# Two attention layers and a mixture of experts on one core: an order of steps computed anew, and three queue details

## The reference

```python
x = L0_attn_x                                    # (2, 1024, 128) float32
x = layernorm(x + attn(x))                       # 8 heads of 16, causal, plus head_scale * q_proj * k_proj
# ffn(x), inside the last line:
#   x = x + mla_attention(rmsnorm(x))            # 16 heads of 8, rotary, latent of 64, causal
#   x = x + moe(rmsnorm(x))                      # argmax over 4 experts, 128 -> 512 -> 128, relu
x = layernorm(x + ffn(x))
```

## Time and profile before

| | us |
|---|---|
| median of 3 runs | 563.38 (559.97 to 565.47) |
| profiled execution | 565.1 |
| its span | 563.4 |
| TensorE busy | 480.2 (85%) |
| VectorE busy | 371.9 (66%) |
| ScalarE busy | 323.6 (57%) |
| mean granted TensorE clock | 0.95 |

### The profile page before, as it was taken

The page is one execution under the profiler, slowest core; times in us unless marked ns, Lnnn a source line. Parts: engine busy times, 40 slices in busy tenths (PEclk is TensorE's granted clock), DMA queues, the critical chain, the costliest instruction groups (busy, mean ns, idle before and its releaser), DMA issues.

```text
span 563.4 us, 10237 instructions
## 1 busy us (share of the span) xinstructions
PE 480.2 (85%) x3749; PEld 223.4 (40%) x3764; DVE 371.9 (66%) x690; ACT 323.6 (57%) x488; POOL 179.8 (32%) x249
## 2 busy tenths in 40 slices
PE   5576799998899989888797998848888988999993
PEld 3242233444442333333232333312554443367762
DVE  4286977788877889688888788866356721233343
ACT  3422156576676668867685776715456677843331
POOL 9830131237554237634030222452202304601000
PEclk9977889999999999999999799976899999999998
DMA  3894030306112002012010102031000000100010
GB/s 96 214 210 132 2 96 23 94 1 243 45 56 65 25 5 83 28 52 65 17 43 9 52 3 58 6 98 45 6 12 15 8 12 20 30 1 0 20 38 20
DMA packets 31571, 28.83 MB, mean 51 GB/s; under 512 B 8017, under 2 KB 27857, under 8 KB 31250
## 3 DMA queue, kind: packets, MB, share of 16 engines
q1 hardware_dynamic: 30626, 26.34, 16.3%
q0 software_dynamic: 896, 1.84, 1.4%
HBM read 19.27 MB, written 9.31 MB: 51 GB/s over the span
## 4 chain that ended last, share of the span: by engine, by line
PE 58%; ACT 10%; DVE 10%; SPq 8%; issue 5%; DMA 4%; POOL 3%; ACTq 1%; another core or an unknown queue 0%; DVEq 0%; POOLq 0%
PE ps L1407 15%; PE ps L1390 10%; ACT pr L1607 7%; PE ps L1370 7%; DVE mparts L1887 6%; PE ps L1486 5%; PE ps L1542 5%; SPq L1018 4%; PE ps L1472 3%; SPq L1088 3%; DMA qs<-nparts 2%; PE ps L1466 2%; PE ps L1586 2%; PE ps L1574 2%; PE ps L1418 2%
## 5 line engine op out<-in xcount | busy, mean ns | idle before, releaser
L1887 DVE TENSOR_REDUCE mparts<-ps 128x2 f32<-128x1024 f32 (+3 forms) x240 | 260.4, 1114 | 83.0 <-PE ps L1370 78.5
L1607 ACT ACTIVATE pr<-ps 128x1024 f32<-128x1024 f32 (+1 forms) x240 | 221.2, 939 | 142.9 <-PE ps L1390 140.6
L1407 PE MATMUL ps<-pr,vs 128*32 128x512 f32 (+3 forms) x1152 | 124.4, 506 | 9.1 <-ACT pr L1607 5.7
L1390 PE MATMUL ps<-qs,ks 64*128 64x512 bf16 (+7 forms) x561 | 102.1, 339 | 21.1 <-DMA qs<-nparts 11.3
L1370 PE MATMUL ps<-ks,qs 61*128 61x512 bf16 (+7 forms) x576 | 108.7, 348 | 4.0 <-DVE mparts L1887 1.9
L1208 POOL TENSOR_SCALAR_AFFINE_SELECT pr<-pr 128x512 f32<-128x512 f32 x96 | 60.7, 635 | 156.5 <-ACT pr L1607 156.3
L1390 PEld LDWEIGHTS ps<-qs,ks 64*128 64x128 bf16 (+1 forms) x576 | 31.5, 96 | 106.7 <-issue 41.6
L1370 PEld LDWEIGHTS ps<-ks,qs 61*128 61x128 bf16 (+1 forms) x576 | 35.5, 101 | 33.3 <-ACT pr L1607 11.0
L1407 PEld LDWEIGHTS ps<-pr,vs 128*32 128x32 f32 x1152 | 23.6, 108 | 48.5 <-issue 30.1
L1711 ACT ACTIVATE work<-ps,b 128x512 f32<-128x512 f32 x32 | 21.8, 685 | 29.7 <-PE ps L1542 28.2
L1363 PE MATMUL ps<-cmask,identb 64*128 64x128 bf16 (+1 forms) x96 | 23.4, 244 | 11.8 <-DVE mparts L1887 4.8
(11 more groups left out here) (174 smaller groups left out, 563.5 us busy)
## 6 DMA issues: line engine op xcount, KB each, us to landing
qs<-scr0q SPq DMA_DIRECT2D x48, 64.0 KB, 2.4
qs<-scr1q SPq DMA_DIRECT2D x84, 32.0 KB
ks<-scr1k SPq DMA_DIRECT2D x84, 32.0 KB
ks<-scr0k SPq DMA_DIRECT2D x36, 64.0 KB, 2.3
scr0q<-parts SPq DMA_DIRECT2D x4, 384.0 KB, 3.1
scr0k<-parts SPq DMA_DIRECT2D x4, 384.0 KB, 3.6
scr1q<-parts SPq DMA_DIRECT2D x4, 384.0 KB, 2.5
scr1k<-parts SPq DMA_DIRECT2D x4, 384.0 KB, 2.7
```

The source lines that it names most:

```text
L1390: last = pe.matmul(to[:, k, h, :], keys(F, 3, 2 * k + h0 + h, j * P, P), queries(F, 3, 2 * k + h0 + h, qb * 512 + lo, n), start=True, stop ...
L1407: last = pe.matmul(ps[VW * h:VW * (h + 1), PVB, lo:lo + n], vs[:, F % VSLOTS, j, VW * h:VW * (h + 1)], pr[:, st % PSLOTS, h, 0:n], start=( ...
L1607: act.activation(heads, scores_at(F, v), ACT.Exp, scale=GROUPS[F][0].scale).then_inc(exped, 1)
L1887: dve.tensor_reduce(heads, maxes_at(F, u), AX_X, ALU.max).then_inc(taken, 1)
```

## The change

- `rows` of the second attention: one transfer writes both halves of the partitions, so 3 transfers in place of 6.
- A load of group F may be planned only behind `rows` of group F - 2.
- Of the first keys' two halves the second is on GpSimd's queue now, the first on SyncE's.
- At most two scatters are open: scatter t waits until scatter t - 2 has landed.
- `tile_out` and `tile_relu` read the tile's expert number into a register ahead of their wait for the step before them, no longer behind it.
- `hidden` c = 0 waits for its input explicitly (its own engine's earlier `gate` had waited for it before).
- Durations, places, weights of the planner and the limit of side banks (3 to 4) are other numbers, so nearly all of the 1401 steps stand elsewhere in the list.

```diff
-MOST = {"scores": 2, "row maxima": 2, "turns": 2, "side": 3}
+MOST = {"scores": 2, "row maxima": 2, "turns": 2, "side": 4}
...
-FIRST = [[(-2.0, -1.5), (-1.6, -1.1)], [(-0.5, 0.0), (-0.1, 0.4)]]
+FIRST = [[(-2.0, -1.5), (-1.6, -1.1)], [(-0.69, -0.19), (0.0, 0.5)]]
...
-URGENT = 0.6
-FEED, BACKLOG = 0.2, 2.0
-SP_IDLE = 5.0
+URGENT = 0.83
+FEED, BACKLOG = 0.36, 3.0
+SP_IDLE = 3.3
...
-         "combine": (DVE, 0.3), "rows": (SP, 1.0), "mask": (POOL, 0.64), "evac": (ACTE, 0.6), "y": (PE, 1.14),
+         "combine": (DVE, 0.3), "rows": (SP, 2.4), "mask": (POOL, 0.64), "evac": (ACTE, 0.59), "y": (PE, 1.14),
...
+def queue_of_load(F, k, half):
+
+    if F == 0 and k == 1:
+        return POOL if half == POOL_HALF else SP
+    return ACTE if F in ON_ACT else SP
...
+POOL_HALF = 1
+ON_ACT = ()
...
         if F >= SLOTS:
-            out.append(("scores", F - SLOTS, NU - 1))
+            out += [("scores", F - SLOTS, NU - 1), ("rows", F - SLOTS + 1, 2)]
...
-            return 48 * (F + 1) + 48 * max(0, F + 1 - ATT[0].groups)
+            return 48 * (F + 1)
...
                     if at.n == 1:
-                        for pair_of in range(2):
-                            row = HALF * (pair_of + 1) - MAXIMA + p
-                            sp.dma_start(qs[row:row + 1, F % SLOTS, 0:2 * T],
-                                         nparts[2 * TB * pair_of:2 * TB * (pair_of + 1), place, p, :]).then_inc(rows_in, 16)
+                        row = HALF - MAXIMA + p
+                        sp.dma_start(qs[row:row + HALF + 1:HALF, F % SLOTS, 0:2 * T], nparts[0:n, place, p, :]).then_inc(rows_in, 16)
...
+                if t >= 2:
+                    pool.wait_ge(scattered[t % 2], 16 * (t // 2))
...
                 elif kind == "hidden":
                     b, i, c = args
+                    if c == 0:
+                        pe.wait_ge(done["feat"], nth("feat", "hat1", b, i))
...
                 elif kind == "tile_out":
                     s, j = args
+                    e = pe.value_load(expert_of[0:1, j:j + 1], min_val=0, max_val=E - 1)
                     pe.wait_ge(done["tile_relu"], nth("tile_relu", s, j))
                     wait_bank(*step)
-                    e = pe.value_load(expert_of[0:1, j:j + 1], min_val=0, max_val=E - 1)
...
                 elif kind == "tile_relu":
                     s, j = args
+                    if j == 0:
+                        act.wait_ge(done["places"], nth("places", s))
+                    e = act.value_load(expert_of[0:1, j:j + 1], min_val=0, max_val=E - 1)
                     act.wait_ge(done["tile_hidden"], nth("tile_hidden", s, j))
                     if j >= 2:
                         act.wait_ge(done["tile_out"], nth("tile_out", s, j - 2))
-                    e = act.value_load(expert_of[0:1, j:j + 1], min_val=0, max_val=E - 1)
```

More of the change, by code:

```diff
@@ L276, in halves_of_load @@
     return (0, 1) if F in HALVED else (2,)
+LOADED_AHEAD = 1.9
 def wanted():
@@ L299, in wanted @@
         for half in halves_of_load(F):
-            add("loads", [(max(-1.05, F - 1.9) + 0.01 * half, ("load", F, k, half)) for k in range(2)])
+            add("loads", [(max(-1.05, F - LOADED_AHEAD) + 0.01 * half, ("load", F, k, half)) for k in range(2)])
     add("loads", [(F - 0.5, ("copy_v", F)) for F in range(NF)])
@@ L356 @@
+         "latent": (PE, 0.97), "lat_copy": (ACTE, 0.38), "lat_moments": (DVE, 1.55), "lat_norm": (ACTE, 1.75),
+         "lat_turn": (PE, 0.58), "lat_feat": (ACTE, 0.77), "square": (ACTE, 0.62), "square_sum": (DVE, 0.7),
+         "hat": (POOL, 1.1), "x12": (POOL, 1.3), "gate": (PE, 0.95), "pick": (DVE, 2.1), "hidden": (PE, 0.88),
+         "relu": (ACTE, 0.68), "expert": (PE, 0.92), "pick_up": (DVE, 1.4), "layer_norm": (DVE, 1.4), "out": (SP, 0.5),
          "copy_v": (POOL, 0.66), "pads": (POOL, 3.6), "ones": (POOL, 4.0), "halves": (POOL, 1.7), "weights": (SP, 5.2), "moe_weights": (SP, 1.1),
@@ L380, in costs @@
     if kind == "load":
-        queue = POOL if step[1:3] == (0, 1) else SP
-        return [(queue, 0.55 * len(PRODUCTS) if queue == POOL else 0.34 * len(PRODUCTS) * (1 + GROUPS[step[1]][0].n))]
+        queue = queue_of_load(*step[1:])
+        return [(queue, 0.55 * len(PRODUCTS) if queue == POOL else (0.47, 0.68)[GROUPS[step[1]][0].n] * len(PRODUCTS))]
     if kind == "b2_parts":
@@ L393, in costs @@
     if kind == "expert" and step[4] == 0:
-        return [(PE, 1.45)]
+        return [(PE, 1.23)]
     return [COSTS[kind]]
@@ L735, in order @@
             end[step] += LANDS_LATER[kind]
-        if step[:3] == ("load", 0, 1):
-            end[step] += POOL_LANDS
+        if kind == "load" and costs(step)[0][0] != SP:
+            end[step] += POOL_LANDS if costs(step)[0][0] == POOL else AFTER_ISSUE[SP]
         if kind == "max":
@@ L895, in build @@
         order_made, rows_set = sem("order_made"), sem("rows_set")
-        scattered, collected_in = sem("scattered"), [sem(f"collected_in{i}") for i in range(2)]
+        scattered, collected_in = [sem(f"scattered{i}") for i in range(2)], [sem(f"collected_in{i}") for i in range(2)]
         sorted_in = [sem(f"sorted_in{p}") for p in range(-(-(TB + E - 1) // PIECES))]
@@ L1054, in sorted_rows @@
                 j = slice(PIECES * p, min(PIECES * p + PIECES, rows_of_tiles(s)))
-                sp.wait_ge(scattered, 16 * len(tokens_of(s)))
+                for n in range(2):
+                    sp.wait_ge(scattered[n], 16 * len(tokens_of(s)) // 2)
                 if p == 0:
@@ L1099, in _ @@
                     store(*args)
-                elif kind == "load" and args[:2] != [0, 1]:
+                elif kind == "load" and queue_of_load(*args) == SP:
                     load(sp, *args)
@@ L1251, in _ @@
                 kind, *args = step
-                if kind == "load" and args[:2] == [0, 1]:
+                if kind == "load" and queue_of_load(*args) == POOL:
                     load(pool, *args)
@@ L1608, in _ @@
                                    scale=GROUPS[F][0].scale).then_inc(exped, 1)
+                elif kind == "load" and queue_of_load(*args) == ACTE:
+                    load(act, *args)
                 elif kind == "evac":
```

18 lines of the change are left out of this document (7 added, 11 removed).

## The result

| | before | after |
|---|---|---|
| median of 4 runs, us | 563.05 (559.97 to 565.47) | 526.76 (524.31 to 528.18) |
| span of the profiled execution | 563.4 | 525.4 |
| TensorE busy | 480.2 | 470.2 |
| TensorE standing still | 83.2 | 55.2 |

The changed kernel takes 0.935 of the time, with an interval of 0.930 to 0.941. I had said 546 us and 535 to 562. Of the 38 us between the two spans 28 are standstill and 10 are busy time. The work is the same (3764 weight loads in both), so I put these 10 down to the clock, whose mean was 0.950 before and 0.971 after.

A forecast was written before the change was run, and what follows sets the result against it. TensorE, busy 85% of the span, was taken as the bound, so order costs time only where it waits or its clock is down. Terms of -4, -4, -6, -1.5, -4 and 0 took 565.1 us to 545.6, said as 546; range 535 to 562.

The forecast's parts named there:

- 1, start: Start: fewer bytes ahead of the first keys and earlier maxima rows, first scores near 43 us; -4 us (0 to -8).
- no-change rival: Whole kernel: what is gained at these places is waited for elsewhere, group 1's maxima come later; about 563 us, 13%.
- 2, three transfers: Maxima rows of eight groups: three transfers instead of six shorten TensorE's waits for them; -4 us (+3 to -5.6).
- term 4: Clock at group 7: the dip follows a wait for maxima that gets 1.6 us shorter; -1.5 us (0 to -3).
- 3, group 9: Group 9, from `places` to its scores: maxima rows issued ahead of a load, shorter hole; -6 us (-1 to -12).
- 5, tiles: Tiles: expert number read ahead of the wait, so 0.78 us before `tile_out` lie beside it; -4 us (0 to -6.8).
- 6, the rest of the order: All other moved steps: same work, TensorE's time filled in the middle, so no gain; 0 us (-6 to +8).
- Slower: Maxima rows of eight groups: each narrow transfer lands late and the clock falls at other groups; 575 us, 5%.
- half-of-it rival: Start stays DMA-bound and VectorE's standstills return at group 9, other gains hold; -10.5 us, 554.6 us, 13%.

The follow-up runs named there:

- order alone: Changed kernel with its three code edits (three transfers, two open scatters, early reads) undone, new planner numbers and rules kept: 538.26 us, ratio 0.955.
- code alone: Kernel before, with its old planner numbers and order, plus the three code edits (three transfers, two open scatters, early reads): 545.82 us, ratio 0.970.

## Why the prediction was wrong, point by point

- **1, start (-4): too small, and by another path.** The first maximum came at 25.94 (I said 26), the issue of the first rows at 39.58 (I said 37.7), the first scores at 46.62 (I said near 43). That is -2.1 at the place I watched. The lead at group 0's cut was 9.3 us, half of it standstill (25.4 to 20.8) and half busy time (70.1 to 65.5 with 428 and 422 weight loads, the clock 0.87 to 0.92). It goes with the second rows, issued 8.1 us sooner. My sum followed the first rows only. The no-change rival had even named the shift that helped, four instead of seven maxima of group 1 ahead of group 0's second ones, and counted it as a loss.
- **2, three transfers (-4): -9.5 in the old order, -7 in the new.** The issue got as short as said (from 3.67 us for six, in the runs above, to 1.59 for three). The landing did not get longer. I priced only TensorE's five waits for the rows; the clock dip of group 7 went with them (term 4, -1.5), and group 9 gained some 3 us more. The sum of 2 and 4 was -5.5. A reading was off too: the 1.76 us of landing in the earlier trace rows begin with the start of the last issue, not behind it.
- **3, group 9 (-6): the place was right.** From `places` to the scores 10.6 us for 17.8, where I built up 12.6 (with 2.1 us of landing, which the earlier trace rows do not have: they give 1.76, the last issue included). VectorE's standstills did not return; the load or the scatters each would have sufficed. The two open scatters, at 0 by me, brought 3.9 us in the old order, where they took the standstill away. In the new order they were not tried alone; of the 11.5 us between order alone and the changed kernel about 2 are left after the other two edits.
- **5, tiles (-4): 6.5 in the old order, 2.6 in the new.** In the old one 5.9 of the 6.8 us of waits at `tile_out` went; in the new one 3.9 of 5.9 went and 1.8 us of "issue" are left. The Trainium skill gives TensorE a queue of 64 instructions ("TensorE: Matmul & The Clock Gate", table of specifications), and from it I had taken that the read would cost nothing, 6.8 us in the sum. The old order comes near that, the new one does not.
- **6, the rest of the order (0): this is the step that failed.** I put it at nothing because the work is the same and TensorE "has 93% of its time filled in the middle". The first is no reason: the same work waited less. The second was misread: between the cuts of groups 0 and 8 TensorE was busy 243.6 of 273.1 us, 89%, and stood still for 29.5. With the order alone it stands still for 17.2 there, with the code alone for 24.2. In time the order alone brought 8.8 us outside the start and group 9, 6.0 of them in groups 1 to 3, where I had no term at all. With the 5.2 us that term 1 was short at the start and the 2.1 us by which the order alone passed term 3 at group 9, that is 16 of the 18.5 us that the sum lacked. What went were many short waits, of which I had summed none but those for the rows.
- **Clock.** TensorE's busy time fell by 10 us. I had 1.5 for group 7 and a bound at group 9. With the missing records counted, the order alone took 5.4 of it (482.0 to 476.6), the code edits on top 4.2 (to 472.4). The order alone still has mean clocks of 0.89 and 0.94 at groups 6 and 7, which are 0.94 and 1.00 after.
- **Slower (5%).** Between 192.5 and 196.6 us the trace after counts 102 packets under 512 bytes for three transfers, 34 each, against 32 each before (192 in six). 32 pieces with 2 more would be two engines, 16 pieces with 16 more would be sixteen. So the trace agrees with the number of engines that the Trainium skill gives ("DMA: Bandwidth & Descriptors", "Why a DMA increments its semaphore by 16 and not by 1"). But the landing took 1.70 us, so the price that I had tied to it was wrong. My 0.075 us a piece, taken from a store of 1 KB pieces, was too much for pieces of 256 bytes.

The half-of-it rival needed VectorE's standstills to return and a start bound by DMA; the DMA share at the start did stay high (83% from 15 to 30 us as before), and the start gained nonetheless. Of the no-change rival nothing came; what I had set against it, 83 us of standstill, was where the gain lay.

## What to carry to other kernels

Before a new order of the same work is priced at nothing, sum the short waits by releaser over the whole middle. Here they were 41 us, 29 of them in 69 waits under a microsecond; the order alone took 16 of the 41, and 14 of the 29. At a start, follow not the first result but the last input of the first group, and count what stands ahead of it on the saturated engine. Numbers of a planner that were chosen together are judged together: returning one set of three cost 11 to 22 us, where all of them with the new code had brought 19.

## What the runs showed of the hardware

- VectorE stood still for 1.5 and 2.6 us at a time, with its input in place as far as the trace shows, while eight indirect scatters ran freely beside 24 loads of 32 KB. Holding scatters to two open, or issuing the loads 10 us later, removed it. Its cause is open.
- A transfer of 8 KB (34 packets, 2 of them of 4 bytes) landed 1.70 us after its issue began, one of 4 KB (32 packets, 16 of them of 4 bytes) in 1.76 and 2.14. These are one chain and two. SyncE's issue took 0.50 us in the median for the first kind and 0.59 for the second.
- The first rows of the start took 4.3 us from the end of issue in the changed kernel and 1.7 in the same order with six transfers later on, where nothing differs up to there. DMA share from 30 to 48 us was 98% in the one and 75% in the other. One profile of this start is uncertain by 2 to 3 us.
